# An attention and expert-routing kernel on eight cores: identity from an iota, V's second half in pieces, K^T V one block later, three weights cast in DRAM

## The reference, cut to what matters

```python
xn = layernorm(x)                               # per token
q, k, v = split(xn @ w_qkv.T + b_qkv)           # 16 heads of 64
q, k = silu(q), softmax(k, axis=tokens)
out = q @ (k.T @ v)                             # per head, no token x token matrix
out = layernorm(out) * ln_g + ln_b
gate = sigmoid((xn @ w_g1.T + b_g1) @ w_g2.T + b_g2)
attn = (out * gate) @ w_out.T + b_out
logits = xn @ Wr.T; top 2 of 8 experts, w = softmax(top 2 values)
# each expert takes at most 769 (token, choice) pairs; pairs beyond that are dropped
ffn[token] = sum over kept choices of w * (xn[token] @ We[expert])
y = x + attn + ffn
```

## Time and profile before

| what | us |
|---|---|
| median of 3 runs | 584.15 |
| lowest, highest | 583.47, 590.22 |
| the profiled execution's own time | 582.3 |
| its span on the slowest core (core 3) | 580.6 |
| spans of the other cores | 560.4 to 579.2 |
| PE matmul busy in the span | 478.1 (82%) |
| DVE, ACT, POOL busy | 291.5, 210.3, 164.2 |

### The profile page before, as it was taken

How to read it: one execution, slowest core, us unless ns; L and a number is a source line. 1 busy time by engine, 2 the same in 40 slices (tenths; PEclk the granted TensorE clock), 3 DMA queues, 4 the chain that set the end, 5 groups by cost and what they waited for, 6 DMA issues and landing times.

```text
span 580.6 us, 9173 instructions; the slowest of 8 cores (560.4 to 580.6 us)
## 1 busy us (share of the span) xinstructions
PE 478.1 (82%) x3104; PEld 241.8 (42%) x3104; DVE 291.5 (50%) x635; ACT 210.3 (36%) x337; POOL 164.2 (28%) x154
## 2 busy tenths in 40 slices
PE   0587999988768879998785876999999958986896
PEld 0253555434334444444333433444445424432342
DVE  3784664067886651356654563421213413634565
ACT  2355444244344533455463553434343323100000
POOL 2253346000064002010004145556658512200000
PEclk9987999999898979999997997999999987999999
DMA  7787953999400989900005447788999996165686
GB/s 197 237 240 213 214 196 64 167 169 170 88 1 27 290 265 166 203 12 1 2 1 105 95 93 180 147 198 193 206 269 253 198 291 262 73 218 172 222 298 251
DMA packets 37829, 96.49 MB, mean 166 GB/s; under 512 B 4432, under 2 KB 4560, under 8 KB 37776
## 3 DMA queue, kind: packets, MB, share of 16 engines
q0 software_dynamic: 18544, 44.37, 39.2%
q1 hardware_dynamic: 15552, 40.92, 22.3%
q10 hardware_dynamic: 3680, 10.52, 4.9%
HBM read 87.74 MB, written 31.46 MB: 205 GB/s over the span
## 4 chain that ended last, share of the span: by engine, by line
PE 55%; DVE 14%; issue 10%; DMA 10%; ACT 6%; SPq 1%; DVEq 1%; ACTq 1%; another core or an unknown queue 1%; PEldq 0%; PEld 0%
PE PS L311 50%; PE PS L315 5%; DMA eo_d<-vq,dtab 5%; DMA wr<-wv_t 4%; DVE bst L880 2%; DVE nm L740 2%; ACT stage L319 2%; DVE stage L330 2%; ACT vq L319 1%; DVE stage L335 1%; SPq L78 1%; DMA wlate<-x_tm 1%; ACT ek L326 1%; DVE wr L330 1%; DVE nb L335 1%
## 5 line engine op out<-in xcount | busy, mean ns | idle before, releaser
L311 PE MATMUL PS<-wr,xnt 128*128 128x512 bf16 x512 | 121.5, 392 | 16.9 <-DVE wr L330 6.2
L311 PE MATMUL PS<-xnt,wr 128*128 128x512 bf16 x512 | 122.4, 386 | 0.5 <-ACT vq L319 0.5
L311 PEld LDWEIGHTS PS<-wr,xnt 128*128 128x128 bf16 x512 | 49.5, 100 | 80.1 <-issue 28.4
L311 PE MATMUL PS<-wlate,stage 128*128 128x512 bf16 x288 | 70.2, 396 | 0.4 <-ACT stage L326 0.4
L311 PEld LDWEIGHTS PS<-xnt,wr 128*128 128x128 bf16 x512 | 48.4, 99 | 51.4 <-issue 4.5
L315 PE MATMUL PS<-ident_sb,vq 128*128 128x128 bf16 x424 | 37.0, 225 | 18.8 <-DMA vq<-xn_d,tabs 6.1
L334 DVE TENSOR_SCALAR vq<-PS,wslot_f 128x512 bf16<-128x512 f32 x24 | 18.0, 751 | 66.9 <-PE PS L311 46.0
L311 PE MATMUL PS<-wr,stage 128*128 128x512 bf16 x224 | 50.6, 379 | 0.5 <-ACT stage L326 0.3
L326 ACT COPY stage<-PS 128x1024 bf16<-128x1024 bf16 x40 | 40.2, 1008 | 23.6 <-PE PS L315 21.2
L330 POOL TENSOR_TENSOR stage<-stage 128x1024 bf16<-128x1024 f32 x16 | 34.0, 2126 | 50.8 <-DVE stage L327 45.0
L315 PEld LDWEIGHTS PS<-ident_sb,vq 128*128 128x128 bf16 x424 | 27.3, 100 | 35.5 <-issue 29.7
(11 more groups left out here) (150 smaller groups left out, 616.8 us busy)
## 6 DMA issues: line engine op xcount, KB each, us to landing
wlate<-x_tm SPq DMA_DIRECT2D x20, 512.0 KB, 8.1
eo_d<-stage SPq DMA_DIRECT2D x4, 2048.0 KB, 17.2
vq<-eo_d SPq DMA_DIRECT2D x16, 512.0 KB, 4.3
xn_d<-stage SPq DMA_DIRECT2D x16, 256.0 KB, 7.3
wlate<-we POOLq DMA_DIRECT2D x2, 2048.0 KB
wr<-we POOLq DMA_DIRECT2D x2, 2048.0 KB, 20.0
wlate<-we POOLq DMA_DIRECT2D x8, 512.0 KB
wr<-x_tm SPq DMA_DIRECT2D x8, 512.0 KB
```

What stands on the lines that cost most here:

```text
L311: return PE.run(lambda e: e.matmul(out, l, r, start=start, stop=stop), *toks, sig=sig)
```

## The change

1. The 128x128 identity is made by an iota and one DVE comparison in place of a DMA.
2. Loads of x: tile 2 waits for tile 1, tile 3 for tile 2; before, tile 3 waited for the last quarter of V's first half (queue of SP), and tiles 0 to 2 went out at once.
3. V's second half is loaded in eight pieces of 256 KB, one per step 1 to 8, cast one per step 3 to 10 on ACT, and staged in `wlate`; V's second half runs 9 tiles behind the first (LAG = 10, was 5 behind). K's weights are loaded in step 8 of `head_loads` and wait for no cast; expert 0's wait for the last cast.
4. K stage: `k_kv` of block j-3 in place of j-2 behind `k_proj(j)`.
5. In the Q stage, b = 0 to 2, the even units issue on POOL twelve casts of 1 MB of float32 from DRAM to 0.5 MB of bf16 in DRAM (experts 6 and 7 and `w_out`, `round_quarter`), each behind its `q_proj`. The three weights are later loaded from there as bf16 by SP's queue.
6. Block 4 and 5: `m_beside` stands ahead of `a_out` and `a_norm` in a unit.
7. Out stage: the lag is 2 for t < 14, then 1.

```diff
@@ loads of x, identity
-            x_tok = {t: load_x(t) for t in range(3)}
+            x_tok = {0: load_x(0)}
+            for t in range(1, 4):
+                x_tok[t] = load_x(t, x_tok[t - 1] if t > 1 else None)
...
-            t_idn = GP.move(counter("c_idn"), ident[:], ident_d)
+            GP.run(lambda e: e.iota(pz_i[:], [[0, 2]], base=0, channel_multiplier=2))
+            a = GP.run(lambda e: e.iota(i_ii[:], [[1, 128]], base=0, channel_multiplier=0))
+            a = tcopy(DV, pz_f[:], pz_i[:], a)
+            t_idn = DV.run(lambda e: e.tensor_scalar(ident[:], i_ii[:], 2.0, pz_f[:, 0:1],
+                                                     op0=ALU.mult, op1=ALU.is_equal), a)
...
-            x_tok[3] = load_x(3, wv_in[0, 3])
@@ V's second half, head loop
+            def wv_piece(c):
+
+                wv_in[1, c] = SP.move(counter(f"c_wvb{c}"), wvf[1][:, c, :],
+                                      wv_t[128 * c:128 * (c + 1), 512:D])
...
-                if t == 6:
-                    late["wk"] = w_load(1, wk_t, stat[t], *[t_wv[1, c] for c in range(HC)])
+                if t == 8:
+                    late["wk"] = w_load(1, wk_t, stat[t])
...
-            for s in range(1, NT + 6):
+            for s in range(1, NT + LAG):
...
-                if s <= 4:
-                    wv_load(SP, 1, s - 1)
-                if s in (4, 5):
-                    for c in range(4 * s - 16, 4 * s - 12):
-                        wv_cast(AC, 1, c)
+                if s <= HC:
+                    wv_piece(s - 1)
+                if 3 <= s < 3 + HC:
+                    wv_cast(AC, 1, s - 3)
...
-                v1 = h_v(s - 6, 1) if s >= 6 else None
+                v1 = h_v(s - LAG, 1) if s >= LAG else None
...
-            load_we(0, 3)
+            load_we(0, 3, t_wv[1, HC - 1])
@@ K stage
-            for j in range(NJ + 2):
-                if j >= 2:
+            for j in range(NJ + 3):
+                if 2 <= j < NJ + 2:
                     k_trans(j - 2)
...
-                if j >= 2:
-                    k_kv(j - 2)
+                if j >= 3:
+                    k_kv(j - 3)
@@ casts in DRAM, weights from there
+            def round_quarter(k, q, *toks):
+                src = (we[E - 2 + k:E - 1 + k, :, :].rearrange("e a b -> (e a) b") if k < 2
+                       else wo_t)
+                rows = slice(256 * q, 256 * (q + 1))
+                rd_tok[k] = GP.move(
+                    c_rd[k], wb_d[k:k + 1, rows, :].rearrange("k a b -> (k a) b"), src[rows, :],
+                    *toks)
...
                 if pending:
-                    slot, q, src, toks = pending.pop(0)
-                    GP.move(c_w[slot], wv3[slot][:, 2 * q:2 * q + 2, :],
-                            src.rearrange("(c p) o -> p c o", p=128)[:, 2 * q:2 * q + 2, :], *toks)
+                    lane, done, slot, q, src, toks = pending.pop(0)
+                    lane.move(done, wv3[slot][:, 2 * q:2 * q + 2, :],
+                              src.rearrange("(c p) o -> p c o", p=128)[:, 2 * q:2 * q + 2, :],
+                              *toks)
...
-                        t_we[e + 6] = quarters(wslot[e], we[e + 6:e + 7, :, :].rearrange(
-                            "e a b -> (e a) b"), freed[e])
+                        t_we[e + 6] = quarters(SP, wslot[e], wb_d[e:e + 1, :, :].rearrange(
+                            "e a b -> (e a) b"), freed[e], rd_tok[e])
@@ blocks
-                    if b < NB:
+                    if b < NB - 1 and u % 2 == 0:
+                        k = 4 * b + u // 2
+                        round_quarter(k // 4, k % 4, q_proj(b, u))
+                    elif b < NB:
...
+                    if b >= NB:
+                        m_beside(b - NB, u)
                     if 1 <= b <= NB:
...
-                    if b >= NB:
-                        m_beside(b - NB, u)
@@ out stage
-                while added <= t - (3 if t < 8 else 2 if t < 12 else 1):
+                while added <= t - (2 if t < NT - 2 else 1):
```

More of the change, by code:

```diff
@@ L187, in build_nc @@
         xnf = [cut(stage, (16 + i * 4) * KB, D, F32) for i in range(2)]
[L188 to L189 removed]
+        wvf = [cut(w, 0, HC * 512, F32).rearrange("p (c o) -> p c o", c=HC)
+               for w in (wring[2], wlate)]
         hot_r = cut(stage, 0, 2 * NT * 128).rearrange("p (i r) -> p i r", r=128)
```

38 lines of the change are left out of this document (19 added, 19 removed).

## The result

The changed kernel takes 560.96 us (median of 4 runs) beside 583.81 for the kernel before on the same chip: ratio 0.9586, 95% interval 0.9499 to 0.9672. It is faster, by 22.9 us where 36.5 were forecast. 560.96 lies in the range given (536 to 566), but not at the forecast of 547.7: it is where the rival "DVE paces head and K stage" put it (561.7). In some executions the cores of one die run at a lower clock and the time is some per cent longer: medians here are of all executions, ratios and intervals of the others alone.

A forecast was written before the change was run, and what follows sets the result against it. PE was taken as the engine to follow, losing time to waits in five stages. Head 6, K stage 8, experts 9.5, block 4 4 and out stage 9 sum to 36.5 us, giving 547.7 us, range 536 to 566.

The forecast's parts named there:

- DVE paces head and K stage: Rival, 20%: head gives 1 us, K stage 3, block 4 nothing; 22.5 us in all, so 561.7 us.
- The out stage: Last stage: lag 2 frees the banks a tile earlier, 3.9 us per tile throughout; 9 us, bounds 5 and 10.
- The experts: Expert stage: bf16 reloads lower the DMA share to 0.76 and end gather waits and the slow clock; 9.5 us, bounds 0 and 13.
- Casts in DRAM: Q stage on: twelve casts at 3.4 us per quarter (1.8 to 5.1), ending near 290 us; price 0.
- the rival: Slower, 4%: casts of T us each hold the gathers due at 330 us; PE waits 12 T - 81 us; 611 at 12 us.
- Head: Head: first loads, V's second half, lag and clock, 2 + 5 - 2.8 + 2 = 6 us; bounds 0 and 9.
- one step 9 instead of 4.1 us: 5 us: Head: ACT's two waits for V's second half and the full four-cast groups made one step long; removing this gains 5 us.
- The first loads: Head: fourth tile of x no longer behind the last weight quarter, 2 us; bounds 0 and 3.
- The lag: Head: second half starts at step 10, not 6; PE idles 0.7 us in each of four steps, price 2.8 us.
- K's and expert 0's weights come two steps later or wait for a cast, both with tens of us to spare: Head: loading these weights later was taken to cost nothing.
- K stage: K loop: `k_kv` one block later removes PE's waits for ACT's copy; 8 us taken, bounds 2 and 15.
- Block 4: Block 4: expert tile covers the normalisation, a pair of tiles falls from 7.17 to about 5.9 us; 4 us, bounds -2 and 6.

The follow-up runs named there:

- run 7: Changed kernel without the casts in DRAM, experts 6 and 7 and `w_out` again loaded as float32 with a cast on POOL's queue: 570.12 us.
- run 8: Changed kernel with the bf16 reloads issued on POOL's software queue in place of SP's: 559.84 us.
- Run 12: Changed kernel with every cast in DRAM done twice, 24 copies instead of 12: 598.63 us.
- run 2: Changed kernel with K's weights loaded at step 12 and not step 8 of the head: 557.43 us, profiled execution alone, no verdict drawn from it.
- run 3: Changed kernel with `k_kv` of block j-2 again in place of j-3: 563.41 us.
- runs 5 and 6: Changed kernel with the routing moved behind the K loop, in the second also `k_kv` of block j-2 again: 583.38 and 592.18 us.
- run 5: Changed kernel with all pieces of the routing taken out of the K loop and done behind it: 583.38 us.
- run 9: Changed kernel with POOL's five `hot_v` products and the table's matmuls moved from the K stage into the Q stage: 557.39 us.
- runs 9 and 10: Changed kernel with POOL's products and table in the Q stage; the second also has DVE's pieces every second block and K's weights later: 557.39 and 555.03 us.
- run 11: Second kernel of runs 9 and 10 with POOL's products held until `kv_sb` is written, table matmuls two units later, DVE's pieces halved, in every block: 547.51 us.

## Why the prediction was right, and where not

**Right: the sign, the range, the two stages behind the casts.** The out stage gained 9.1 us of 9; its edit was not undone alone, but it is the only one there, and the tiles follow each other in 3.95 us from the start. The experts gained 8.0 on average and 11.2 on the slowest core, of 9.5; run 7 puts 7.7 of the mean over the cores down to the casts. No gather wait is left on any core and no clock near 0.5 in that stage. The DMA share is 0.82 where 0.76 was forecast: the forecast took the 20 us of casting quarters out of the 82 and put nothing in for the reloads, and three quarters of `w_out` at 1.8 us fall there, 5.3 us. Nor did `w_out` come as "four DMAs at once": its quarters stand between loads of x in SP's queue and went out at 390.0, 411.6, 413.7 and 431.7 us on core 2. Nothing waited for them. One reason given was wrong: "gathers and scatters no longer stand behind weights in their queue" is worth nothing (run 8); the halved bytes are all of it.

**Casts in DRAM: mis-sized, harmless.** 4.8 us per quarter and not 3.4, inside the bounds of 1.8 and 5.1. They ended at 313 and not near 290; price 0, as run 7 shows. The estimate from the Trainium skill ("DMA: Bandwidth & Descriptors", Where 436 GB/s comes from) was nearer: 53 us for the twelve, 58 measured. A quarter moves 1.57 MB at the HBM, 327 GB/s against its 358. Run 12 measures the rival: 24 copies delay the gathers by 41 us, where the rule in the forecast (12 T - 81, T = 9.6) gave 34.

**Head: 6 forecast, 0.2 measured.** The normalisations split it (starts in us, means of the cores, from ACT's timelines):

| | before | after | gain |
|---|---|---|---|
| third | 25.2 | 24.7 | 0.5 |
| third to sixth | 13.3 | 13.0 | 0.3 |
| sixth to seventh | 9.5 | 4.3 | 5.2 |
| seventh to eleventh | 20.1 | 17.2 | 2.9 |
| eleventh to last | 23.9 | 26.2 | -2.3 |
| last to the first maximum | 24.1 | 30.5 | -6.4 |

The term "one step 9 instead of 4.1 us: 5 us" came, with 5.2. Three other steps failed. The first loads were given 2 us and gave 0.5. The lag was given a price of 2.8 us and the clock a gain of 2: the price is four second halves at the end, 7.0 us, less the 4.2 that four steps of 4.07 in place of 5.12 would give back. The end did grow by 6.4 us, but the steps and the clock together gave back 2.9 and not 6.2. And "K's and expert 0's weights come two steps later or wait for a cast, both with tens of us to spare" was true of who needs them and not of who stands beside them: K's weights delay a tile of x to 14.16 us, and from the eleventh normalisation to the last it takes 26.2 us, with these weights four steps later 22.6 (run 2). DVE's waits for x are 3.4 us before, 10.5 after and 4.7 in run 2 (core 2). The first K matmul was to come at 109 and came at 115. What a smaller lag with the pieces would give, no run shows.

**K stage: 8 forecast, 2.8 measured (3.0 by run 3).** The step is "I take 8". The mechanism was right (10.5 us in runs 5 and 6), and the doubt stood beside it: "there DVE sets the pace, and a wait removed from PE returns as another". What the forecast did not price was the last clause of that sentence, POOL's 15.8 us. The loop is a ladder of four runs:

| what stands in the loop | us |
|---|---|
| PE's own work (run 5) | 70.0 |
| and DVE's routing pieces (run 9) | 79.4 |
| and POOL's products (changed kernel) | 89.1 |
| and `k_kv` of block j - 2 (run 3) | 92.1 |

The third rung, 9.7 us, agrees with the 10.2 us that four DVE instructions stood behind POOL. The kernel before had it too, 5.9 us, and the row that sums the stage (56.6 of 76 busy) hid it, because an instruction that stands still counts as busy. So the move of `k_kv` also changed which DVE instructions meet POOL's products, and the stall grew by 4.2 us. It can be a part of why only 3 of the 10.5 us came; no run holds the stall fixed and moves `k_kv` alone.

The Trainium skill has the rule ("SBUF — State Buffer", Who interferes with whom): DVE and GpSimd share a pair of ports as an exclusive lock. A DVE instruction with two inputs in SBUF blocks against a GpSimd instruction that reads SBUF, and one in a two-port mode, which `tensor_scalar` can enter, blocks too; a reduction does not. The trace agrees on who waits (`zw` and `kv_sb` with two inputs, `sr` as a `tensor_scalar`) and who does not (the maxima, 0.68 us throughout). The page states the lock for one instruction, and in the changed kernel DVE came in between POOL's products; in runs 9 and 10 it stood for all five, 15.75 to 15.95 us, on all eight cores of both.

**Block 4: 4 forecast, nothing measured.** The step is "7.17 becomes about 5.9". 0.5 us of each pair came, and the stage is no shorter, because the waits changed their name: on core 2 PE waited 0.72, 1.38, 1.37 and 1.43 us for normalisations before, 4.9 in all, and after it 0.98, 0.90 and 0.90 for `z` and 1.96 for the last normalisation, 4.7. DVE's work per pair was given as 5.6 us from means; that it comes in an order, with z's operation behind statistics and normalisation, was left out.

**The rival.** "DVE paces head and K stage" gave head 1, K 3, block 4 nothing: 22.5 us. Measured are 0.2, 2.8 and -1.1, and its total is met. In part this is luck. For the K stage it was right in part, since half of what DVE lacks is POOL's doing. In the head the normalisations did come 6.6 us earlier, and the lag took it back behind them, which is no matter of DVE's pace.

**Open.** Why the loop stays at 79 us with DVE's pieces in it, whether whole in every block, whole in every second, or halved (79.4, 78.9, 79.0). The 8 to 10 us of waits are for the exponential behind a late maximum. And why run 11's Q stage with the table is 3.8 us longer than the changed kernel's (98.8 against 95.0).

## What to carry to other kernels

When an engine's busy share makes it the suspect, look at the longest instance of its small instructions beside their usual length: 3 us for a product of four columns is another engine's time, and here moving that engine's work away was worth more to the loop (9.7 us) than reordering PE (3). When a change brings a gain and a price, give each its own mark and its own run: undoing both at once shows nothing but their sum. Ask of every load not when it is needed but what it stands beside. Casting weights once in DRAM, in a stretch with idle DMA engines, pays where a later stage is bound by bytes; its limit is the first thing behind it in the same queue.

## What the runs showed of the hardware

- A copy with a cast from DRAM to DRAM (1 MB of float32 to 0.5 MB of bf16, eight cores at once) takes 4.8 us with 97.8% of the core's 16 DMA engines to itself; PE waited 41 us for the gather behind 24 of them.
- A load of 4 MB issued at 53.97 us and landed 29.2 us later stood beside a 0.5 MB tile of x that took 14.16 us; issued four steps later it lets the head end 2.3 to 3.3 us earlier.
- A DVE instruction of four columns stood 15.75 us beside five POOL products of 3.18 us that followed one another without a gap (runs 9 and 10, began 0.05 us behind the first on core 2 of run 9); where DVE came into the sequence 0.75 us after its start, it stood for single products (2.46, 2.52, then two `kv_sb` in 6.01 us).
- The expert stage takes as long with the bf16 reloads on the software queue as with them on SP's (126.6 us both).
